# Rotated cross attention of a four-layer decoder: keys prepared in the layer before, inverse roots as GpSimd powers, queries rotated before they are scaled

## What is computed

```python
def _L0_attn_ref(hidden_states, ...):
    ...
    o = i * jnp.sum(c * g, axis=-1, keepdims=True)
    o = rms_norm(o, nout, EPS_OUT)
    return bit_linear(o, Wo, no)          # rms norm, quantise to 8 bits, ternary weights

def _L0_xattn_ref(q, k, v, Wq, Wk, Wv, Wo, q_norm_w, k_norm_w):
    def _rms_norm(x, w):                  # over the 8 numbers of one head
        return w * x * jax.lax.rsqrt(jnp.mean(x * x, axis=-1, keepdims=True) + EPS)
    ...
    query, key_, value = (proj(q, Wq), proj(k, Wk), proj(v, Wv))
    query = _rms_norm(query, q_norm_w)
    key_ = _rms_norm(key_, k_norm_w)
    query = query * cos + _rotate_half(query) * sin
    key_ = key_ * cos + _rotate_half(key_) * sin
    scores = jnp.einsum('bhqd,bhkd->bhqk', query, key_) * scale
    ...                                   # causal mask, softmax, times value
    return attn @ Wo.T
```

## Time and profile before

| | before |
|---|---|
| median of 3 runs (lowest to highest) | 756.54 us (756.26 to 758.4) |
| the profiled execution: time, span | 757.45 us, 755.7 us |
| mean granted TensorE clock | 0.879 of full speed |
| PE busy | 597.1 us (79%) |
| DVE busy | 485.1 us (64%) |
| ACT busy | 245.6 us (33%) |
| POOL busy | 119.1 us (16%) |
| share of the chain that ended last | PE 70%, DVE 21%, POOL 4%, ACT 3% |

### The profile page before, as it was taken

One profiled execution on the slowest core, in us unless ns is written; L12 is line 12 of the kernel. 1 busy time (PEld: TensorE's weight loads), 2 busy tenths in 40 slices (PEclk: granted clock), 3 DMA queues, 4 the chain that ended last, 5 costly groups with the idle time before them and its releaser, 6 DMA issues.

```text
span 755.7 us, 10867 instructions
## 1 busy us (share of the span) xinstructions
PE 597.1 (79%) x4297; PEld 392.8 (52%) x4305; DVE 485.1 (64%) x1288; ACT 245.6 (33%) x361; POOL 119.1 (16%) x118
## 2 busy tenths in 40 slices
PE   2314599976999899969977878998779869996486
PEld 1314255676455645656665755556435554564335
DVE  7788777677588666753354536785654547766685
ACT  2342134414334333334414332344221032443150
POOL 5023510014210131010010014200200061102110
PEclk9657579979899999987997799899799977999678
DMA  9600000000000000000000000000000000000000
GB/s 314 279 0 1 0 1 2 1 1 2 0 2 1 1 1 2 1 1 1 1 0 1 1 1 0 1 2 1 1 0 1 0 1 1 1 2 0 1 0 29
DMA packets 6722, 12.42 MB, mean 16 GB/s; under 512 B 528, under 2 KB 4880, under 8 KB 6288
## 3 DMA queue, kind: packets, MB, share of 16 engines
q1 hardware_dynamic: 6672, 11.73, 4.3%
HBM read 11.21 MB, written 0.52 MB: 16 GB/s over the span
## 4 chain that ended last, share of the span: by engine, by line
PE 70%; DVE 21%; POOL 4%; ACT 3%; issue 2%; POOLq 0%; DVEq 0%; ACTq 0%
PE ps L410 52%; PE ps L473 11%; PE ps L491 3%; PE ps L426 3%; DVE st L1106 2%; DVE xn L1278 2%; POOL rs L324 2%; DVE x L1208 1%; DVE mv L1109 1%; DVE big L1194 1%; DVE mx L1188 1%; ACT td L846 1%; PE ps L578 1%; ACT big L866 1%; PE ps L699 1%
## 5 line engine op out<-in xcount | busy, mean ns | idle before, releaser
L1188 DVE TENSOR_REDUCE mx<-ps 128x8 f32<-128x1024 f32 x80 | 98.0, 1225 | 60.9 <-PE ps L410 60.8
L866 ACT ACTIVATE big<-ps 128x1024 f32<-128x1024 f32 x80 | 81.9, 1023 | 139.7 <-PE ps L473 139.7
L1194 DVE TENSOR_TENSOR big<-ps,mx 128x1024 f32<-128x1024 f32 x80 | 97.7, 1221 | 4.3
L410 PE MATMUL ps<-KTm,qk 32*128 32x512 f32 x320 | 96.3, 682 | 0.0
L473 PE MATMUL ps<-kt,big 128*128 128x128 f32 x640 | 89.4, 285 | 4.6 <-DVE big L1194 4.5
L324 POOL TENSOR_TENSOR rs<-ve,negh 128x4 f32<-128x4 f32 x26 | 26.6, 1023 | 414.0 <-DVE ve L1111 414.0
L473 PEld LDWEIGHTS ps<-kt,big 128*128 128x128 f32 x640 | 72.6, 145 | 26.7 <-DVE big L1194 14.0
L410 PE MATMUL ps<-xnT,wt 128*128 128x512 f32 (+1 forms) x148 | 76.9, 658 | 3.1 <-DVE big L1467 3.1
L410 PE MATMUL ps<-wt,big 128*128 128x128 f32 (+1 forms) x480 | 61.0, 280 | 0.0
L410 PEld LDWEIGHTS ps<-wt,big 128*128 128x128 f32 (+1 forms) x480 | 56.4, 191 | 8.0 <-issue 6.0
L410 PEld LDWEIGHTS ps<-big,vaug 128*32 128x32 f32 x1280 | 30.4, 109 | 48.0 <-ACT big L866 30.3
(11 more groups left out here) (261 smaller groups left out, 790.9 us busy)
## 6 DMA issues: line engine op xcount, KB each, us to landing
wt<-in_weights SPq DMA_DIRECT2D x1, 1664.0 KB, 16.8
wt<-in_weights SPq DMA_DIRECT2D x1, 1603.0 KB, 11.5
wt<-in_weights SPq DMA_DIRECT2D x6, 256.0 KB, 10.6
bt<-in_bconsts SPq DMA_DIRECT2D x1, 1024.0 KB, 7.9
rowt<-in_rows SPq DMA_DIRECT2D x1, 975.0 KB, 5.5
wt<-in_weights SPq DMA_DIRECT2D x1, 832.0 KB, 13.0
wt<-in_weights SPq DMA_DIRECT2D x1, 608.0 KB, 18.1
wt<-in_weights SPq DMA_DIRECT2D x1, 580.0 KB, 5.7
```

Source lines behind the costliest of these rows:

```text
L410: return pe.matmul(out, lhsT, rhs, start=start, stop=stop, **k)
L866: act.activation(half, heads_of(pair(g, u)), ACT.Exp, scale=SCALES[l]).then_inc(*s.step(f"exp{u}"))
L1188: dve.tensor_reduce(top, S, AX.X, ALU.max).then_inc(*s.step())
L1194: dve.tensor_tensor(pr[:, half * HH:(half + 1) * HH, :].rearrange("p (i j) k -> p i j k", i=2), S, top.unsqueeze(3).to_broadcast([P, 2, HG ...
```

## The change

Keys: k's projection, its squares, the copy to td, the mean per head and the power run inside L0a (phases 12.5 and 13 of layer 1) instead of in L0x. `rotate_keys` of group 0 runs on GpSimd in L0a's phase 13, that of group 1 in L0x's phase 0.5, behind the powers for xn. The transposes of the rotated keys have a function of their own, at L0x's phase 1 for group 0 and 5 for group 1, and VectorE's masked copy of the first keys runs at phase 3 for group 0 and behind the queries for group 1. k now goes through bank 2, and TensorE waits at phase 12.5 of L0a for the weights of L0x. Inverse roots: the Newton steps are gone, and GpSimd takes a power -0.5 of 128x64 numbers, once for k and once for q of each group. Queries: `rotate` reads them from the accumulator unscaled, and one multiplication with the inverse roots follows. TensorE's first scores move from phase 20 to phase 8, behind the transposes of the group's own queries. GpSimd's masked copies wait for the rotated queries of both groups. L3a's instructions stay as they are.

```diff
+                        if l == "L0x":
+                            for other in range(GROUPS):
+                                pool.wait_ge(*s.at("L0x.qrot", other))
...
-            def rotate_keys(n, l):
-
-                yield n, 6
+            def inverse_root(m, name):
+
+                part = slice(m * GB * H, (m + 1) * GB * H)
+                pool.wait_ge(*s.at(f"{s.layer}.{name}"))
+                pool.tensor_tensor(t.y2[:, part], t.v2[:, part], negh[:, 0:1].to_broadcast([P, GB * H]), ALU.pow).then_inc(*s.step(name + "_r"))
+
+            def rotate_keys(l):
+
                 heads = GB * H
                 raw = t.ta[:, GB:2 * GB, :].rearrange("p b (h d) -> p (b h) d", h=H)
                 new = t.td[:, :, :].rearrange("p b (h d) -> p (b h) d", h=H)
                 tmp = t.tb.rearrange("p b (h d) -> p (b h) d", h=H)
                 pool.wait_ge(*s.at(f"{l}.kraw"))
-                if l == "L0x":
+                if l == "L0a":
                     pool.wait_ge(*p.at("pre.gwT"))
-                    pool.wait_ge(*s.at("L0x.y2"))
+                    pool.wait_ge(*s.at("L0a.kv_r"))
                     pool.tensor_tensor(raw, new, t.y2[:, heads:2 * heads].unsqueeze(2).to_broadcast([P, heads, HD]), ALU.mult).then_inc(*s.step())
...
+                    yield n, 13
+                    inverse_root(1, "kv")
+                    if g == 0:
+                        rotate_keys(l)
...
-                if l in ("L0x", "L3a"):
-                    yield from rotate_keys(n, l)
+                if l == "L0x":
+                    if g == GROUPS - 1:
+                        yield n, 0.5
+                        s.begin("L0a")
+                        rotate_keys("L0a")
+                        s.begin(l)
+                    yield n, 6
+                    inverse_root(0, "qv")
+                if l == "L3a":
+                    yield n, 6
+                    rotate_keys(l)
...
-                yield n, 20
+                yield n, (8 if l == "L0x" else 20)
...
+            def turn_keys():
+
+                pe.wait_ge(*s.at("L0a.x"))
+                pe.wait_ge(*s.at("L0a.krot"))
+                turn_rows(1, t.td, "KTp")
...
-                        pe.wait_ge(*s.at("L0a.x"))
-                        project_rows(1, ctxT, w("L0x_wk"), "k")
+                        pe.wait_ge(*s.at("L0a.kraw"))
                     else:
                         project_cols(1, ctxT, w(f"{l}_wk"), "k")
                     project_rows(2, ctxT, w(f"{l}_wv"), "v")
+                    if l == "L0x" and g == 0:
+                        yield n, 1
+                        turn_keys()
...
+                    yield n, 12.5
+                    pe.wait_ge(*s.at("L0a.ctxT"))
+                    if g == 0:
+                        pe.wait_ge(loaded["L0x"], 16)
+                    pe.wait_ge(*s.at("L0a.ms1"))
+                    project_rows(2, ctxT, w("L0x_wk"), "k")
                     yield n, 14
-                    pe.wait_ge(*s.at("L0a.ctxT"))
...
+                    if l == "L0x" and g == GROUPS - 1:
+                        yield n, 5
+                        turn_keys()
                     yield n, 8
                     pe.wait_ge(*s.at(f"{l}.qrot"))
                     turn_rows(0, t.tc, "QTp")
-                    pe.wait_ge(*s.at(f"{l}.krot"))
-                    turn_rows(1, t.td, "KTp")
-                    yield n, 20
+                    if l == "L3a":
+                        pe.wait_ge(*s.at("L3a.krot"))
+                        turn_rows(1, t.td, "KTp")
+                    yield n, (8 if l == "L0x" else 20)
...
                     values()
+                    if g == 0:
+                        read(KT, bank(1), "KTp", "KT")
...
+                    yield n, 12.5
+                    act.wait_ge(*s.at("L0a.k"))
+                    act.activation(t.ta[:, GB:2 * GB, :], four(bank(2)), ACT.Square).then_inc(*s.step("ksq"))
+                    read(t.td[:, :, :], four(bank(2)), "k", "kraw")
...
-                        for m, nm in ((1, "k"), (0, "q")):
-                            act.wait_ge(*s.at(f"L0x.{nm}"))
-                            act.activation(t.ta[:, m * GB:m * GB + GB, :], four(bank(m)), ACT.Square).then_inc(*s.step(f"{nm}sq"))
-                        read(t.td[:, :, :], four(bank(1)), "k", "kraw")
+                        act.wait_ge(*s.at("L0x.q"))
+                        act.activation(t.ta[:, 0:GB, :], four(bank(0)), ACT.Square).then_inc(*s.step("qsq"))
+                        if g == GROUPS - 1:
+                            yield n, 6
+                            read(KT, bank(1), "KTp", "KT")
...
+            def mean_of_heads(m, name):
+
+                part = t.v2[:, m * GB * H:(m + 1) * GB * H]
+                dve.tensor_reduce(part, ta[:, m * GB:m * GB + GB, :].rearrange("p b (h d) -> p (b h) d", h=H), AX.X, ALU.add).then_inc(*s.step())
+                dve.wait_ge(*s.last())
+                dve.tensor_scalar(part, part, 1.0 / HD, 1e-10, ALU.mult, ALU.add).then_inc(*s.step(name))
...
-                if l in ("L0x", "L1a", "L3a"):
+                if l in ("L1a", "L3a"):
                     yield n, 19
-                    dve.wait_ge(*s.at(f"{l}.KT"))
-                    dve.tensor_tensor(t.KTm[:, 0, :, :], keys_of(t, 0), own_head(), ALU.mult).then_inc(*s.step("keys0"))
+                    first_keys(l)
...
+                    yield n, 12.5
+                    dve.wait_ge(*s.at("L0a.ksq"))
+                    mean_of_heads(1, "kv")
...
-                    v2, y2, h2, hh = t.v2, t.y2, t.h2, GB * H
+                    if g == 0:
+                        yield n, 3
+                        first_keys(l)
                     yield n, 6
-                    dve.wait_ge(*s.last())
-                    for m, nm in ((0, "q"), (1, "k")):
-                        dve.wait_ge(*s.at(f"L0x.{nm}sq"))
-                        v = ta[:, m * GB:m * GB + GB, :].rearrange("p b (h d) -> p (b h) d", h=H)
-                        dve.tensor_reduce(v2[:, m * hh:(m + 1) * hh], v, AX.X, ALU.add).then_inc(*s.step())
-                    dve.wait_ge(*s.last())
-                    dve.tensor_scalar(v2[:, :], v2[:, :], 1.0 / HD, 1e-10, ALU.mult, ALU.add).then_inc(*s.step())
-                    dve.wait_ge(*s.last())
-                    dve.tensor_scalar(h2[:, :].bitcast(I32), v2[:, :].bitcast(I32), 1, None, ALU.logical_shift_right).then_inc(*s.step())
-                    dve.wait_ge(*s.last())
-                    dve.tensor_scalar(y2[:, :].bitcast(I32), h2[:, :].bitcast(I32), -1.0, float(0x5F3759DF), ALU.mult, ALU.add).then_inc(*s.step())
-                    dve.wait_ge(*s.last())
-                    for _ in range(3):
-                        dve.tensor_tensor(h2[:, :], y2[:, :], y2[:, :], ALU.mult).then_inc(*s.step())
-                        dve.wait_ge(*s.last())
-                        dve.scalar_tensor_tensor(h2[:, :], h2[:, :], -0.5, v2[:, :], ALU.mult, ALU.mult).then_inc(*s.step())
-                        dve.wait_ge(*s.last())
-                        dve.scalar_tensor_tensor(y2[:, :], h2[:, :], 1.5, y2[:, :], ALU.add, ALU.mult).then_inc(*s.step("y2"))
-                        dve.wait_ge(*s.last())
-                    v = ta[:, 0:GB, :].rearrange("p b (h d) -> p (b h) d", h=H)
-                    dve.tensor_tensor(v, bank(0).rearrange("p (h d) -> p h d", d=HD), wide(y2[:, 0:hh], HD), ALU.mult).then_inc(*s.step())
-                    dve.wait_ge(*s.last())
-                    rotate(v, cw[0][:, :], sw[0][:, :], tc, "qrot", "half")
+                    dve.wait_ge(*s.at("L0x.qsq"))
+                    mean_of_heads(0, "qv")
+                    rotate(bank(0).rearrange("p (h d) -> p h d", d=HD), cw[0][:, :], sw[0][:, :], tc, "qraw", "half")
+                    dve.wait_ge(*s.at("L0x.qv_r"))
+                    new = tc[:, :, :].rearrange("p b (h d) -> p (b h) d", h=H)
+                    dve.tensor_tensor(new, new, wide(t.y2[:, 0:GB * H], HD), ALU.mult).then_inc(*s.step("qrot"))
+                    if g == GROUPS - 1:
+                        first_keys(l)
```

More of the change, by code:

```diff
@@ L147, in __init__ @@
             self.sq = own("sq", [P, 3, GB])
-            self.v2, self.y2, self.h2 = (own(n, [P, 2 * GB * H]) for n in ("v2", "y2", "h2"))
+            self.v2, self.y2 = (own(n, [P, 2 * GB * H]) for n in ("v2", "y2"))
             qk = own("qk", [P, 2 * W4])
@@ L933, in program @@
                     read(QT, bank(0), "QTp", "QT")
-                    read(KT, bank(1), "KTp", "KT")
+                    if l == "L3a":
+                        read(KT, bank(1), "KTp", "KT")
                     yield from attend(n, l)
@@ L1162, in rotate, with first_keys @@
                 dve.wait_ge(*s.last())
+            def first_keys(l):
+                dve.wait_ge(*s.at(f"{l}.KT"))
+                dve.tensor_tensor(t.KTm[:, 0, :, :], keys_of(t, 0), own_head(), ALU.mult).then_inc(*s.step("keys0"))
             def attend(n, l):
```

## The result

The changed kernel takes 776.82 us (776.06 to 777.82) against 757.04 us before, a ratio of 1.026 with a 95% interval of 1.024 to 1.028: 19.8 us slower. The forecast was 742.0, faster. The profiled execution has a span of 775.1 us (755.7 before) at a mean granted clock of 0.878 (0.879).

What follows compares the result with a forecast made beforehand. Bound: a TensorE-VectorE wait chain from 57 to 94 us, 20.0 of it VectorE alone. Terms +1.7, -0.5, -11.8, -3.4 make -14.0, with the clock's -1.5 -15.5: from 757.45 to 742.0 us, range 738 to 746.5.

Steps and rivals of the forecast that it cites:

- Part 4: GpSimd's queue of key and query powers and key rotations: one power taken as 1.15 us, costing nothing below about 2.2.
- p: Time of one GpSimd power of 128x64 numbers, taken as 1.15 us, with bounds of 1.15 and 16.3 us.
- by the count: Rival: GpSimd's power costs by the count of numbers, 16.3 us each, first round at 136.6, 800 us; chance 0.10.
- 71.4 + 4p: Start in us of the first attention round if GpSimd is last everywhere, with p the time of one power.
- The rivals' formula: First attention round at 71.4 us plus four times one GpSimd power, once GpSimd is last everywhere.
- Part 1: Keys moved into L0a: two means of heads on VectorE ahead of phase 13, +1.7 us for everything behind.
- contention during L0a's end: Term of the forecast's range: GpSimd and VectorE sharing SBUF interfaces there could make it 1.0 us later.
- Parts 2 and 3: L0x: TensorE ahead of queries, ready at 67.4 us, -0.5; VectorE's queries 4.4 and 3.8 us, 8.2 for 20.0, -11.8.
- Part 5: Earlier first scores on TensorE: 4.2 us a group, first round at 80.2 for 94.2 us, leg 4.6 for 8.0.
- Part 6: TensorE's clock at the first attention rounds: two slow rounds cost 2.7 us, an earlier rise gains 1.5 us.
- The range: Forecast itself 738 to 746.5 us; 737 to 751 takes in the clock and blocks rivals, not the count.

Runs made afterwards that it cites:

- p_short4: The changed kernel with its four GpSimd powers taking only the first 4 of 64 numbers per partition, other inverse roots left at 1: 746.98 us.
- r_late: The changed kernel with powers of 4 numbers, other roots left out, and first scores of both groups back in phase 20: 750.44 us.
- p_sizes: The kernel before plus a row of GpSimd powers of different sizes in the third layer's idle stretch, output unchanged: 755.23 us, one execution.
- q_dummy: The kernel before plus five scratch multiplications of 128x512 on GpSimd behind its last small power of the first layer: 761.67 us.
- q_sqrt_behind: The changed kernel with roots by ScalarE square root and VectorE reciprocal, and GpSimd's key rotations only after xn of both groups: 745.19 us.
- q_sqrt: The changed kernel with each inverse root as a ScalarE square root and a VectorE reciprocal, no large GpSimd power: 748.04 us.

## Why the prediction was wrong, point by point

**Part 4, the step that failed: the size of p.** "I take 1.15, since the only two sizes measured cost the same." p is 10.5 us. The row of 16x1 was the one support for a flat cost, and it was a disturbed one: 0.54 us undisturbed. With 0.54 for one number and 1.01 for four, the two rows give a slope of 0.157 us a number and 10.4 us for 64. Had the first row been read together with VectorE's cast beside it, or been distrusted because one value is no series, the count would have been the likeliest case. The upper bound, 16 x 1.02 = 16.3, held; the rival "by the count" had the mechanism and the sign, and its deciding point, p = 5.7, is passed. Its time of 800 is too high, because of the 0.38 that is paid only once.

A smaller slip stands beside it. "Below about 2.2 us p costs nothing" comes from 71.4 + 4p = 80.2, where GpSimd is last everywhere. By the part's own times, group 1's rotation done at 69.7 and the power wanted at 70.8, it is 1.1 us. Measured: no wait at 1.0 us and 1.1 us of it, twice, at 2.9.

**The rivals' formula.** 71.4 + 4 x 10.53 = 113.5 us for the first round; 114.4 was measured. That p stands four times on the path, twice before the power for xn and twice before the multiplications, was right. That the number fits so well is partly luck. The formula lets GpSimd run on from the power for xn through group 1's rotation to q's power, 8.0 us. The chain goes another way: through VectorE's xn, held to 4.63 us, TensorE's projection, the square and the mean, 10.2 us from 76.75 to 86.91, while GpSimd is idle for the last 2.8. Group 0's rotation, with VectorE almost idle, took 5.1 us instead of 5.9 and made up a part.

**Part 1, sized wrongly for the case p is small.** The means and squares cost what was said: phase 13 starts at 51.4 us in the changed kernel, +1.5 for +1.7. But "contention during L0a's end" stood in the range with 1.0 us. With short powers it is 3.4 us until x and 2.5 more in xn. The rule was named and then applied to the large products only, not to the small instructions between them, whose count and not size decides. So even with p = 1 the forecast would have missed by 5: 747.0 against 742.0, outside its range of 738 to 746.5.

**Parts 2 and 3.** q was ready at 74.2 us in p_short4, not at 67.4: 5.9 us by part 1, and 0.9 because TensorE transposed and projected in 2.6 us (0.88 + 1.72) where part 2 took 1.7 at full clock. VectorE's two groups then took 3.6 us each (74.2 to 77.8 and 77.8 to 81.35), against 4.4 and 3.8: right for the second, 0.8 too high for the first, since GpSimd's rotation was over by then (72.6).

**Part 5** was right: TensorE took 3.8 and 3.9 us for the two groups' transposes and scores, for 4.2 each, and its leg from group 1's queries to the first round was 4.2 us in p_short4 (81.35 to 85.56) for 4.6. Of the 3.4 that the leg was to lose, 1.1 are the keys' transposes; r_late shows 2.7 us for the order of the scores where that leaves 2.3.

**Part 6** can't be confirmed. In p_short4 the first two rounds took 6.5 us (85.56 to 92.02) and in the profiled kernel before 8.9, 2.4 us for the 1.5 that was taken; but p_sizes took 5.2 us with the instructions of before. In the medians little of it is left: 9.4 us gained, of which 8.6 are the first round. And the cost of the two slow rounds was read too low: they were compared with the later 3.09 us, which hold matrix products with v that the first two don't have. At full clock these take 2.52 and 2.65 us, so the slow clock cost 3.7 us, not 2.7.

**The range** left out what happened, a case that had been given 0.10.

## What to carry to other kernels

A flat pair of rows at small sizes doesn't exclude a slope; measure one instruction of the size that is wanted before a queue is built around it, and look at what ran beside a row before it is used as a price. When work is moved to GpSimd beside VectorE, count VectorE's instructions that read two SBUF tensors, and its tensor_scalars on SBUF, not their bytes: each can wait until a GpSimd instruction of over 1 us ends, and moving the rotation from one stage to another moved this loss with it. A queue position is priced by everything behind it: here the power counted four times, with xn of the next layer among those that waited.

## What the runs showed of the hardware

- GpSimd's power of fp32 numbers costs 0.38 us plus 0.158 us for each number of a partition, the same for 16 and 128 partitions (0.54 for 1 number, 1.63 for 8), for the values 0.7, 50, 1e-6 and 1, and for a broadcast or a whole tile of exponents (0.54 for 1, 1.01 for 4, 10.5 for 64). A multiplication of 128x512 costs 1.04: for each number the power is about 80 times dearer. The Trainium skill's GPSIMD Engine Reference, section 3.1, gives 2.6 cycles an element for a two-input instruction at 1.2 GHz; by this clock 0.158 us are about 190 cycles (an estimate), so it holds for no power here.
- A VectorE tensor_scalar or two-input instruction on 128x4 took 0.89 to 1.23 us instead of 0.16 to 0.23 beside GpSimd's multiplications and additions of 128x512 (p_short4, q_dummy), and 0.17 beside GpSimd's power. In q_sqrt_behind a reciprocal of 128x64 (0.55) and products with one input in the accumulator (0.68) took there what they take beside an idle GpSimd.
- TensorE's clock rose at different instants in two executions with the same instructions (granted 0.50 from 94 to 98 us before, 1.00 in p_sizes), with the third transposes 4.4 us apart and the times 2.2 us.
- A square root of 128x64 on ScalarE took 0.26 us and a reciprocal on VectorE 0.56, so an inverse root costs 0.8 us there for GpSimd's 10.5, besides a table load of 1.28 us that ran in ScalarE's idle time (q_sqrt).
